# A fused attention and ternary-FFN layer: moving the weight-magnitude sums from the attention phase to ScalarE's queue in the projection phases, and reading the projection banks earlier

## The chip, the cores and the metric

The kernel runs as one program on all 8 cores of a Trainium2 chip. Each core works alone on its share of the tokens (1024 of 8192 query rows); the cores exchange nothing. The metric is the device time of the slowest core in microseconds (us).

## The reference, cut to what matters

`x` is 2 sequences of 4096 tokens with 2048 features, f32.

```python
xn = layernorm(x)
# attention, 16 heads of 128
q, k, v = xn @ Wq.T, xn @ Wk.T, xn @ Wv.T
q = layer_norm_per_head(q * gamma + beta) * 128**-0.5
k = layer_norm_per_head(k * gamma + beta)
attn = where(causal, (q @ k.T) ** 2, 0)
o = (attn @ v) / (attn.sum(-1) + EPS);  attn_out = o @ Wo.T
# FFN with ternary weights and int8-like activations
def bit_linear(x, w, g):
    xq = quantize(rms_norm(x, g))            # 127 / max|x| per row
    wq = clip(round(w / mean(|w|)), -1, 1) * mean(|w|)
    return xq @ wq.T
gate, up = split(bit_linear(xn, gate_w, 1));  h = silu(gate) * up
out = x + attn_out + bit_linear(h, down_w, 1)
```

The one scalar mean(|w|) of each FFN matrix must be known before its weights can be made ternary. That takes a pass over all of `gate_w` (23 M numbers) and `down_w` (11.5 M numbers): the kernel reads them in 264 chunks of 128 x 1024 f32 (512 KB each) and sums the absolute values of each chunk into a column of `wabs_g` or `wabs_d`. These chunks ("abs chunks" below) are what the change moves.

## The kernel before, in words

The program is written with raw engine queues. `V`, `SC` and `TE` (lines 159 to 168) append an instruction to VectorE (DVE), ScalarE (ACT) or TensorE (PE), and each engine runs its queue strictly in the order in which the Python code appended to it. Data passes by semaphores: `cV`, `cS` and `cT` count finished instructions of DVE, ACT and PE. So the order in the source is the schedule, by hand.

The phases, with a barrier between each:

- Phase 1 (32 tiles `t` of 128 tokens, the whole sequence). PE: 16 transposes of the normalised tile into `xnT` (`pe_transposes`, L339), the K projection (`proj_mm`, L364: 4 PSUM banks `kv_ps`, 16 matmuls of 128x512 each), 16 transposes of the K heads of the tile before (`head_transposes_store`, L416), and the V projection into the same four banks. K and V share the banks, so the V projection's first matmul waits until DVE has read bank 0 of K (L374, `kg <- kv_ps * gmb`), and the next K projection's banks are free when ACT has copied V out (L478).
- DVE and ACT in phase 1: `ln_tile` (L299 to L322) normalises tile t+1; `featuremap` (L374 to L400) reads the K banks, adds beta, makes squares on ACT (L380), the per-head statistics, a root on ACT (L393) and 16 scalings into `kfm`. The K heads' transposes are copied out alternately by ACT (L423) and DVE (L427) into two store buffers `ktb`, each of which must first have been stored to DRAM (`ksc`).
- `emit_abs(n)` (L264 to L285) takes the next n abs chunks: a DMA on POOL's queue into one of two buffers `wfp`, issued when that buffer's last reader has finished, and the sum, on ACT as an Abs with accumulation (L283, each followed by a read of the accumulator), or, with `dve=True`, on DVE as a reduction (L278). In phase 1 it is called twice a tile with 2 chunks: 4 a tile, 128 in all.
- Phase 2 (8 own tiles `s`): the same for Q with `wk_sb` reloaded with Wq, then an RMS norm and quantisation of the tile for the FFN (L544 to L568), stored through the same head transposes. `emit_abs` is called with 3, 3 and 2 chunks a tile: 64 in all.
- Phase 3: attention, for C = 0 (16 key blocks a head, all masked) and C = 1 (32 key blocks, the last 16 masked), over 16 heads. Per block: scores on PE (L642), the square on ACT (L653, or L664 unmasked), the mask on DVE (L655) if masked, and two matmuls (L670 for the output, L674 for the row sums). After each head ACT and DVE divide (L680, L683, L684), and then `emit_abs(3, dve=True)` stands on DVE's queue until the last 72 chunks are used: after the 16 heads of C = 0 and the first 8 of C = 1.
- Then Wo, gate and up with ternary weights, quantisation, and down. The change doesn't touch these.

Of the kernel before, what the change touches and what calls it, by code (L numbers as in the profile page):

```python
# [100 lines left out]
def build_nc():  # L101
# [57 lines left out]
    def V(fn, waits=(), drain=True):  # L159
        w = list(waits) + ([(cV, cV.n)] if drain else [])  # L160
        return b.op("vector", fn, waits=w, inc=cV)
# [5 lines left out]
    def TE(fn, waits=(), inc=True):  # L167
# [54 lines left out]
           for i in range(2)]  # L222
# [4 lines left out]
    wv_sb = es_wv.enter_context(nc.sbuf_tensor("wv_sb", [128, 16 * DM], BF16,  # L227
                                               side="right"))
# [35 lines left out]
    def emit_abs(n, dve=False):  # L264
        for _ in range(n):
            i = abs_i[0]
            if i >= len(abs_chunks):
                return
            abs_i[0] = i + 1
            src, which, col = abs_chunks[i]  # L270
            slot = i % 2
            en, val = abs_sc_ck[slot]
            b.dma("gpsimd", wfp[slot][:], src, s_abs[slot],
                  waits=[(CTR[en], val)])
            tgt = wabs_g if which == 0 else wabs_d
            if dve:
                abs_sc_ck[slot] = ("cV", V(
                    lambda e, sl=slot, t=tgt, cc=col: e.reduce_sum(  # L278
                        t[:, cc:cc + 1], wfp[sl][:], axis=AX.X,
                        apply_absolute_value=True), waits=[s_abs[slot]]))  # L280
            else:
                abs_sc_ck[slot] = ("cS", SC(
                    lambda e, sl=slot, t=tgt, cc=col: e.activation(  # L283
                        wabs_dump[:], wfp[sl][:], ACT.Abs,
                        accum_out=t[:, cc:cc + 1]), waits=[s_abs[slot]]))  # L285
# [83 lines left out]
            cks.append(cT.n)  # L369
        return cks  # L370

    def featuremap(dst_bf, q_scale, mm_cks, dst_waits):
        for j in range(4):
            v = V(lambda e, jj=j: e.tensor_tensor(  # L374
                kg[:, jj * 512:(jj + 1) * 512], kv_ps[jj][:],
                gmb[:, jj * 512:(jj + 1) * 512], ALU.mult),
                waits=[(cT, mm_cks[j]), (s_misc, ck_misc0)])
            st["kv_evac"][j] = ("cV", v)
        V(lambda e: e.tensor_add(kg[:], kg[:], btb[:]))  # L379
        sck = SC(lambda e: e.activation(kg2[:], kg[:], ACT.Square),  # L380
                 waits=[(cV, cV.n)])
        V(lambda e: e.reduce_sum(
            st1.ap().rearrange("p (h o) -> p h o", o=1),
            kg.ap().rearrange("p (h d) -> p h d", h=H), axis=AX.X))
        V(lambda e: e.reduce_sum(
            st2.ap().rearrange("p (h o) -> p h o", o=1),
            kg2.ap().rearrange("p (h d) -> p h d", h=H), axis=AX.X),
          waits=[(cS, sck)])
        V(lambda e: e.tensor_single_scalar(st1[:], st1[:], 1.0 / HD, ALU.mult))
        V(lambda e: e.tensor_single_scalar(st2[:], st2[:], 1.0 / HD, ALU.mult))  # L390
        V(lambda e: e.tensor_tensor(st3[:], st1[:], st1[:], ALU.mult))
        vck = V(lambda e: e.tensor_tensor(st2[:], st2[:], st3[:], ALU.subtract))
        sck = SC(lambda e: e.activation(st3[:], st2[:], ACT.Sqrt, bias=EPS),  # L393
                 waits=[(cV, vck)])
        V(lambda e: e.reciprocal(st3[:], st3[:]), waits=[(cS, sck)])
        if q_scale:
            V(lambda e: e.tensor_single_scalar(st3[:], st3[:], DSC, ALU.mult))
        last = 0
        for h in range(H):
            last = V(lambda e, hh=h, d=dst_bf: e.tensor_scalar(  # L400
                d[:, hh * 128:(hh + 1) * 128], kg[:, hh * 128:(hh + 1) * 128],
                st1[:, hh:hh + 1], st3[:, hh:hh + 1], ALU.subtract, ALU.mult),
                waits=(list(dst_waits) if h == 0 else ()), drain=(h == 0))
        return last
# [40 lines left out]
    kfm_ring = [kfm, kfm2]  # L445
# [4 lines left out]
    for t in range(NT):  # L450
        slot = t % 2
        if t + 1 < NT:
            nslot = (t + 1) % 2
            vf, sf = st["xf_free"][nslot]
            b.dma("sync", xf[nslot][:], xfull[(t + 1) * 128:(t + 2) * 128, :],
                  s_x[nslot], waits=[(cV, vf), (cS, sf)])
        pe_transposes(xnb[slot], [xnT[:, g * 512:(g + 1) * 512] for g in range(4)],
                      first_waits=[(cT, st["xnT_free"]), (cV, st["xn_ck"][t])])
        st["xnb_free"][slot] = [(cT, cT.n)]
        xnT_ready = [(cV, cV.n), (cS, cS.n)]  # L460
        kck = proj_mm(wk_sb, first_waits=[(s_w, ck_winit)] + xnT_ready)
        if pend1[0] is not None:
            pfm = pend1[0]
            head_transposes_store(kfm_ring[(t - 1) % 2], pfm,
                                  lambda h, tt=t - 1: ksc[h, :, tt, :])
            kfm_free2[(t - 1) % 2] = [(cT, cT.n)]
        emit_abs(2)
        if t + 1 < NT:
            st["xn_ck"][t + 1] = ln_tile(xf[(t + 1) % 2], want_f32=False,
                                         xslot=(t + 1) % 2)  # L470
        fm_ck = featuremap(kfm_ring[slot], q_scale=False, mm_cks=kck,
                           dst_waits=kfm_free2[slot])
        pend1[0] = fm_ck
        vck_banks = proj_mm(wv_sb, first_waits=[])
        st["xnT_free"] = vck_banks[-1]
        emit_abs(2)
        for j in range(4):
            v = SC(lambda e, jj=j, xs=slot: e.copy(  # L478
                xnb[xs][:, jj * 512:(jj + 1) * 512], kv_ps[jj][:]),
                   waits=[(cT, vck_banks[j])])  # L480
            st["kv_evac"][j] = ("cS", v)
        sck = cS.n
        for h in range(H):
            b.dma("sync", vsc[h, :, t, :], xnb[slot][:, h * 128:(h + 1) * 128],
                  s_kvw[slot], waits=([(cS, sck)] if h == 0 else []))
        st["xnb_free"][slot] = [(s_kvw[slot], s_kvw[slot].n)]
    head_transposes_store(kfm_ring[(NT - 1) % 2], pend1[0],
                          lambda h: ksc[h, :, NT - 1, :])
    kfm_free2[(NT - 1) % 2] = [(cT, cT.n)]
# [23 lines left out]
    for s in range(NOWN):  # L513
# [9 lines left out]
        xnT_ready = [(cV, cV.n), (cS, cS.n)]  # L523
        qck = proj_mm(wk_sb, first_waits=[(s_w, ck_wq)] + xnT_ready)
        st["xnT_free"] = qck[-1]
        emit_abs(3)
        if pend[0] is not None:
            pslot, pqb, pfm = pend[0]
# [8 lines left out]
        if s + 1 < NOWN:  # L537
            st["xn_ck"][s + 1] = ln_tile(xf[(s + 1) % 2], want_f32=True,
                                         xslot=(s + 1) % 2,
                                         xn_dst=xn_f[(s + 1) % 2])  # L540
        fm_ck = featuremap(kfm_ring[slot], q_scale=True, mm_cks=qck,
                           dst_waits=kfm_free2[slot])
        emit_abs(3)
        sck = SC(lambda e, xs=slot: e.activation(kg2[:], xn_f[xs][:],  # L544
# [23 lines left out]
        qb_ck = V(lambda e, xs=slot: e.tensor_copy(xnb[xs][:], xq8[:]),  # L568
                  waits=[(cT, xnT_tr_ck)])
        pend[0] = (slot, qb_ck, fm_ck)  # L570
        emit_abs(2)
    pslot, pqb, pfm = pend[0]
    head_transposes_store(kfm_ring[pslot], pfm,
                          lambda h: qsc[h, :, NOWN - 1, :])
# [43 lines left out]
    for C in range(2):  # L618
# [5 lines left out]
        for h in range(H):  # L624
# [62 lines left out]
                waits=[(cS, sck), (cT, zstop)])  # L687
            oz_free[h % 2] = vck
            rz_free = vck
            emit_abs(3, dve=True)  # L690

    assert abs_i[0] == len(abs_chunks), abs_i[0]

# [563 lines left out]
```

How the kernel before makes its waits and increments, by code:

```python
        def f(eng, wl=wl, fn=fn, ih=ih, inc_n=inc_n, drain=drain):  # L67
            for h, v in wl:
                if v > 0:
                    eng.wait_ge(h, v)
            if drain:
                eng.drain()
            ins = fn(eng)
            if ih is not None:
                ins.then_inc(ih, inc_n)
# [9 lines left out]
        def f(eng, wl=wl):  # L85
            for h, v in wl:
                if v > 0:
                    eng.wait_ge(h, v)
# [6 lines left out]
            def f(eng, h=bar.h, t=target):  # L95
                eng.sem_inc(h, 1)
                eng.wait_ge(h, t)
```

## Time and profile before

| what | value |
|---|---|
| median of the runs | 4940.29 us (4912.0 to 4968.58, 2 runs) |
| the profiled execution | 4851.61 us |
| its span (core 7, the slowest) | 4850.1 us |
| all cores' spans | 4817.5 to 4850.1 us |
| PE busy | 2984.8 us, 62% of the span |
| DVE busy | 1933.9 us, 40% |
| ACT busy | 1734.1 us, 36% |

The profile shows one execution on its slowest core. Busy shares are averages over phases with different limits, so the phases have to be read apart. In a line of the timeline the two first numbers are start and duration in us, then engine, line, operation and tiles, and in square brackets the idle time of that engine just before, with what ended it. PE matmuls are pipelined: 64 projection matmuls at TensorE's full clock take 13.97 us.

### The profile page before, as it was taken

To read this page: it belongs to the slowest core of one execution; us is meant where nothing else is said; L and a number is where in the kernel's file an instruction comes from. 1 tells how busy PE (TensorE), PEld (TensorE's weight loads), DVE (VectorE), ACT (ScalarE), POOL (GpSimd) and SP (SyncE) were. 2 spreads that over 40 slices of the span, in tenths; PEclk is the share of its full clock that TensorE was granted. 3 is DMA by queue.
4 is the path that set the end of the run, shared out by engine and by line. 5 is a ranking of instruction groups with operands and counts; after the bars stand their busy time and mean duration, and the time that the engine had idled before them with its cause. 6 is when DMAs were issued, how large, how long until landed. Compare 5 with 4: busy or idle time off the path is not lost.

```text
span 4850.1 us, 52075 instructions; the slowest of 8 cores (4817.5 to 4850.1 us)
## 1 busy us (share of the span) xinstructions
PE 2984.8 (62%) x13416; PEld 1244.3 (26%) x13416; DVE 1933.9 (40%) x3488; ACT 1734.1 (36%) x2541; POOL 241.1 (5%) x452
## 2 busy tenths in 40 slices
PE   0767676766767232332455567776899989313888
PEld 0333232333333111110111122222344434111333
DVE  0434444353443245443333233213366666332221
ACT  0322222232222123223333455552244444453551
POOL 1000000000000100000000000000000000000000
PEclk9988888888889665666778899998999999655999
DMA  9333333333333633223333323114477676445886
GB/s 173 84 94 88 92 92 83 94 89 96 88 87 84 146 89 98 76 85 107 93 92 95 112 96 117 56 56 131 141 233 235 230 229 201 145 148 170 285 283 188
DMA packets 312716, 628.19 MB, mean 130 GB/s; under 512 B 181872, under 2 KB 194160, under 8 KB 280432
## 3 DMA queue, kind: packets, MB, share of 16 engines
q0 software_dynamic: 64512, 310.41, 22.3%
q1 hardware_dynamic: 247920, 314.45, 21.0%
q8 instruction: 123, 2.02, 0.2%
q14 instruction: 161, 1.32, 0.1%
HBM read 573.34 MB, written 84.93 MB: 136 GB/s over the span
## 4 chain that ended last, share of the span: by engine, by line
PE 36%; DVE 19%; ACT 15%; DMA 13%; issue 10%; another core or an unknown queue 3%; SPq 3%; DVEq 1%; ACTq 1%; POOL 0%; POOLq 0%
PE kv_ps L364 19%; PE ops L670 4%; ACT s2t L653 3%; DMA xob<-xown 3%; DMA hgr<-hgscr 2%; SPq L80 2%; ACT sgn L758 2%; ACT sgn L761 2%; DVE s2t L655 2%; PE gps L909 2%; PE zps L674 2%; PE sps L642 2%; PE wops L830 2%; PE ups L921 2%
## 5 line engine op out<-in xcount | busy, mean ns | idle before, releaser
L364 PE MATMUL kv_ps<-wv_sb,xnT 128*128 128x512 bf16 x2048 | 516.3, 419 | 356.7 <-DVE kg L374 356.7
L364 PE MATMUL kv_ps<-wk_sb,xnT 128*128 128x512 bf16 x2560 | 579.4, 388 | 170.1 <-DMA wv_sb<-wvt 89.0
L670 PE MATMUL ops<-s2t,vsb 128*128 128x512 bf16 x768 | 304.5, 397 | 392.2 <-DVE s2t L655 342.6
L653 ACT ACTIVATE s2t<-sps 128x512 bf16<-128x512 f32 x512 | 305.8, 597 | 434.4 <-PE sps L642 422.7
L655 DVE TENSOR_TENSOR s2t<-s2t,msk_sb 128x512 bf16<-128x512 bf16 x512 | 217.4, 425 | 564.1 <-ACT s2t L653 559.8
L909 PE MATMUL gps<-terng,xqs 128*128 128x512 bf16 x1408 | 343.9, 401 | 74.3 <-DVE ternu L777 58.1
L364 PEld LDWEIGHTS kv_ps<-wv_sb,xnT 128*128 128x128 bf16 x2048 | 214.3, 106 | 648.5 <-issue 454.1
L364 PEld LDWEIGHTS kv_ps<-wk_sb,xnT 128*128 128x128 bf16 x2560 | 252.3, 100 | 485.2 <-issue 204.0
L427 DVE COPY sgn<-tp_ps 128x512 bf16<-128x512 bf16 x96 | 40.8, 424 | 842.3 <-PE tp_ps L416 592.1
L1134 PE MATMUL dps<-dtern,hqts 128*128 128x512 bf16 x1408 | 325.2, 394 | 65.7 <-DMA hqts<-hqtd 62.0
L642 PE MATMUL sps<-qsb,ksb 128*128 128x512 bf16 x768 | 304.6, 399 | 42.2 <-DMA qsb<-qsc 42.1
L423 ACT COPY sgn<-tp_ps 128x512 bf16<-128x512 bf16 x96 | 56.3, 586 | 761.8 <-PE tp_ps L416 573.1
L921 PE MATMUL ups<-ternu,xqs 128*128 128x512 bf16 x1408 | 318.3, 379 | 0.0
L674 PE MATMUL zps<-s2t,ones_bf 128*128 128x512 bf16 x768 | 306.2, 399 | 0.0
L283 ACT ACTIVATE sgn<-wfp 128x1024 bf16<-128x1024 f32 x192 | 203.0, 1057 | 215.7 <-DMA wfp<-gwt_r 184.9
L339 PE MATMUL tp_ps<-ident,xnb 128*128 128x128 bf16 x640 | 56.5, 236 | 362.1 <-ACT xnT L345 192.2
L670 PEld LDWEIGHTS ops<-s2t,vsb 128*128 128x128 bf16 x768 | 74.8, 97 | 667.2 <-issue 666.0
L909 PEld LDWEIGHTS gps<-terng,xqs 128*128 128x128 bf16 x1408 | 143.1, 102 | 262.5 <-issue 113.4
L1134 PEld LDWEIGHTS dps<-dtern,hqts 128*128 128x128 bf16 x1408 | 140.1, 101 | 250.6 <-issue 100.6
L1062 PE MATMUL tp<-ident,hgb 128*128 128x128 bf16 x352 | 51.3, 300 | 245.1 <-DVE hgb L1038 175.5
L80 POOL DMA_DIRECT2D wfp<-gwt_r x176 | 96.8, 553 | 1910.5 <-ACT sgn L283 1905.5
L380 ACT ACTIVATE kg<-kg 128x2048 f32<-128x2048 f32 x40 | 76.5, 1912 | 314.9 <-DVE kg L379 314.9
(139 smaller groups left out, 3597.3 us busy)
## 6 DMA issues: line engine op xcount, KB each, us to landing
wfp<-gwt_r POOLq DMA_DIRECT2D x176, 512.0 KB, 4.8
wfpt<-gwt_r POOLq DMA_DIRECT2D x88, 1024.0 KB, 6.1
wfp<-dwt_r POOLq DMA_DIRECT2D x88, 512.0 KB, 4.1
xqs<-xqsc SPq DMA_DIRECT2D x88, 512.0 KB, 4.3
wfpt<-dwt_r POOLq DMA_DIRECT2D x44, 1024.0 KB, 7.6
hqts<-hqtd SPq DMA_DIRECT2D x32, 1408.0 KB, 8.5
xf<-xfull SPq DMA_DIRECT2D x32, 1024.0 KB, 5.5
hgscr<-hgb SPq DMA_DIRECT2D x88, 256.0 KB, 2.4
```

What stands on the lines that cost most here:

```text
L80: return self.op(engine, lambda e, o=out, i=in_: e.dma_start(out=o, in_=i), waits=waits, inc=sem, inc_n=16)
L283: lambda e, sl=slot, t=tgt, cc=col: e.activation(wabs_dump[:], wfp[sl][:], ACT.Abs, accum_out=t[:, cc:cc + 1]), waits=[s_abs[slot]]))
L364: TE(lambda e, jj=j, f=fc, w=w_sb: e.matmul(kv_ps[jj][:], xnT[:, f * 128:(f + 1) * 128], w[:, f * DM + jj * 512: f * DM + (jj + 1) * 512], ...
L642: TE(lambda e, sl=slot, vv=v, bb=sb: e.matmul(sps[bb][:], ksb[sl][:, vv * 128:(vv + 1) * 128], qsb[sl][:], start=True, stop=True), waits=w ...
L653: sck = SC(lambda e, bb=sb: e.activation(s2t[bb][:], sps[bb][:], ACT.Square), waits=[(cT, mm_ck)])
L655: vck = V(lambda e, bb=sb, vv=v: e.tensor_tensor(s2t[bb][:], s2t[bb][:], msk_sb[:, (vv % 16) * 512:((vv % 16) + 1) * 512], ALU.mult), wait ...
L670: TE(lambda e, sl=slot, vv=v, bb=sb, hh=h, n=NC: e.matmul(ops_[hh % 2][:], vsb[sl][:, vv * 128:(vv + 1) * 128], s2t[bb][:], start=(vv == 0 ...
L674: TE(lambda e, vv=v, bb=sb, hh=h, n=NC: e.matmul(zps[hh % 2][:], ones_bf[:], s2t[bb][:], start=(vv == 0), stop=(vv == n - 1)), inc=(v == N ...
L758: SC(lambda e, w=wv: e.activation(sgn[0][:], w, ACT.Sign, bias=th_m[:, 0:1]), waits=[s_gw[slot], (cV, sgn_free[0])] + list(extra))
L909: TE(lambda e, f=fc, r=ring, bb=pb, xs=xslot: e.matmul(gps[bb][:], xqs[xs][:, f * 128:(f + 1) * 128], terng[r][:, f * 512:(f + 1) * 512], ...
L921: TE(lambda e, f=fc, r=ring, bb=pb, xs=xslot: e.matmul(ups[bb][:], xqs[xs][:, f * 128:(f + 1) * 128], ternu[r][:, f * 512:(f + 1) * 512], ...
L1134: TE(lambda e, f=fc, h_=hs, bb=pb, r=ring: e.matmul(dps[bb][:], hqts[h_][:, f * 128:(f + 1) * 128], dtern[r][:, f * 512:(f + 1) * 512], st ...
```

## The change

Three edits:

1. The reading of the four projection banks (L374) is split off from `featuremap` as `featuremap_evac`. In phase 1 it now stands on DVE's queue ahead of `ln_tile` of the next tile, in phase 2 directly behind the Q projection and ahead of the head transposes' copies.
2. The abs chunks of phase 1 become 6 a tile: the 2 ahead of `ln_tile` are gone, the 2 behind the V projection stay, and 4 are added at the end of the tile, behind the four V copies. In phase 2 they become 3, 3 and 3.
3. The 72 DVE sums in phase 3 are gone (32 x 6 + 8 x 9 = 264 is all of them).

```diff
-    def featuremap(dst_bf, q_scale, mm_cks, dst_waits):
+    def featuremap_evac(mm_cks):
         for j in range(4):
             v = V(lambda e, jj=j: e.tensor_tensor(
                 kg[:, jj * 512:(jj + 1) * 512], kv_ps[jj][:],
                 gmb[:, jj * 512:(jj + 1) * 512], ALU.mult),
                 waits=[(cT, mm_cks[j]), (s_misc, ck_misc0)])
             st["kv_evac"][j] = ("cV", v)
+
+    def featuremap(dst_bf, q_scale, dst_waits):
         V(lambda e: e.tensor_add(kg[:], kg[:], btb[:]))
...
# phase 1, tile t
-        emit_abs(2)
+        featuremap_evac(kck)
+        vck_banks = proj_mm(wv_sb, first_waits=[])
+        st["xnT_free"] = vck_banks[-1]
         if t + 1 < NT:
             st["xn_ck"][t + 1] = ln_tile(xf[(t + 1) % 2], want_f32=False,
                                          xslot=(t + 1) % 2)
-        fm_ck = featuremap(kfm_ring[slot], q_scale=False, mm_cks=kck,
+        fm_ck = featuremap(kfm_ring[slot], q_scale=False,
                            dst_waits=kfm_free2[slot])
         pend1[0] = fm_ck
-        vck_banks = proj_mm(wv_sb, first_waits=[])
-        st["xnT_free"] = vck_banks[-1]
         emit_abs(2)
...
         st["xnb_free"][slot] = [(s_kvw[slot], s_kvw[slot].n)]
+        emit_abs(2)
+        emit_abs(2)
# phase 2, tile s
         st["xnT_free"] = qck[-1]
+        featuremap_evac(qck)
         emit_abs(3)
...
         pend[0] = (slot, qb_ck, fm_ck)
-        emit_abs(2)
+        emit_abs(3)
# phase 3, end of a head
             rz_free = vck
-            emit_abs(3, dve=True)
```

PE's, SP's and POOL's queues hold the same instructions in the same order as before, but that POOL issues 192 of the abs loads ahead of the reload of `wk_sb`, not 128. Lines behind 374 are numbered 2 to 5 higher in the changed kernel.

ACT in phase 1, one tile from the root of `featuremap` (L393, then L395) to the root of the next tile's. L283 are the abs chunks, L478/L480 the V copies, L345 the copies of the transposed tile `xnT`, L423/L425 those of the K heads. Before:

```order
L393 ACTIVATE st<-st 128x16
L283 ACTIVATE sgn,wabs_g<-wfp 128x1024 x2
L478 CAST xnb<-kv_ps 128x512 x4
L345 COPY xnT<-tp_ps 128x512 x2
L423 COPY sgn<-tp_ps 128x512 x2
L283 ACTIVATE sgn,wabs_g<-wfp 128x1024 x2
L299 ACTIVATE xnb,lnst<-xf 128x2048
```

and in the changed kernel:

```order
L395 ACTIVATE st<-st 128x16
L283 ACTIVATE sgn,wabs_g<-wfp 128x1024 x2
L480 CAST xnb<-kv_ps 128x512 x4
L283 ACTIVATE sgn,wabs_g<-wfp 128x1024 x4
L345 COPY xnT<-tp_ps 128x512 x2
L425 COPY sgn<-tp_ps 128x512 x2
L299 ACTIVATE xnb,lnst<-xf 128x2048
```

Four chunks now stand between the V copies and the copies of `xnT`, on which the next K projection waits; none stands ahead of `ln_tile` (L299) any more.

DVE in phase 1, the same tile from the K heads' copies (L427, then L429) to the add of beta (L379, then L381). Before:

```order
L427 COPY sgn<-tp_ps 128x512 x2
L302 TENSOR_REDUCE lnst<-xf 128x1
...
L322 TENSOR_SCALAR xnb<-xf,lnst 128x2048
L374 TENSOR_TENSOR kg<-kv_ps,gmb 128x512 x4
L379 TENSOR_TENSOR kg<-kg,btb 128x2048
```

and in the changed kernel:

```order
L429 COPY sgn<-tp_ps 128x512 x2
L374 TENSOR_TENSOR kg<-kv_ps,gmb 128x512 x4
L302 TENSOR_REDUCE lnst<-xf 128x1
...
L322 TENSOR_SCALAR xnb<-xf,lnst 128x2048
L381 TENSOR_TENSOR kg<-kg,btb 128x2048
```

The four readings of the K banks have passed the seven instructions of `ln_tile`.

DVE in phase 3, C = 0, one head: L655 (then L660) are the 16 masks of a head, L684 (then L689) its division. Before:

```order
L655 TENSOR_TENSOR s2t<-s2t,msk_sb 128x512 x16
L684 TENSOR_TENSOR O_sb<-ops,sgn 128x512
L278 TENSOR_REDUCE wabs_d<-wfp 128x1 x3
```

and in the changed kernel:

```order
L660 TENSOR_TENSOR s2t<-s2t,msk_sb 128x512 x16
L689 TENSOR_TENSOR O_sb<-ops,sgn 128x512
```

The three sums between a head's division and the next head's first mask are gone.

## Rows read from the trace of the kernel before

**Rows 1.** Phases 1, 2, 3 (C = 0): busy PE, PEld, DVE, ACT, POOL, PEclk, DMA, GB/s.

```profile
117.00:1580.00 1463.00, 1021.11 (x5025) 466.19 (x5026) 646.01 (x1209) 424.76 (x655) 67.73 (x125) 0.87 0.33 89
...
1700.00:2200.00 500.00, 151.99 (x784) 73.56 (x784) 230.33 (x395) 138.78 (x218) 33.71 (x59) 0.62 0.30 87
2200.00:2716.00 516.00, 239.99 (x792) 65.47 (x792) 185.53 (x332) 178.63 (x298) 24.78 (x47) 0.78 0.31 93
```

**Rows 2.** The chain that ended last, four projections of 64 matmuls: start, duration.

```profile
151.39 13.97 PE kv_ps L364 x64
...
836.86 16.94 PE kv_ps L364 x64
...
1558.45 13.97 PE kv_ps L364 x64
...
1868.16 16.69 PE kv_ps L364 x64
```

**Rows 3.** Waits in phase 1: total us, times, longest us.

```profile
PE kv_ps L364 <- DVE kg L374: 356.7, 31, 13.2
```

**Rows 4.** The timeline of one tile of phase 1.

```profile
801.06 1.06 ACT L283 ACTIVATE sgn<-wfp 128x1024 bf16<-128x1024 f32 x1 [0.20 <-ACT st L393]
802.76 0.53 POOL L80 DMA_DIRECT2D wfp<-gwt_r  x1 [17.76 <-ACT sgn L283]
803.54 1.93 ACT L478 CAST xnb<-kv_ps 128x512 bf16<-128x512 f32 x3
806.60 0.59 ACT L478 CAST xnb<-kv_ps 128x512 bf16<-128x512 f32 x1 [1.12 <-PE kv_ps L364]
...
807.25 7.50 SPq L80 DMA_DIRECT2D vsc<-xnb  x16
807.38 0.59 ACT L345 COPY xnT<-tp_ps 128x512 bf16<-128x512 bf16 x1 [0.19 <-PE tp_ps L339]
...
809.67 13.97 PE L364 MATMUL kv_ps<-wk_sb,xnT 128*128 128x512 bf16 x64 [0.96 <-DVE xnT L349]
...
829.69 0.42 DVE L427 COPY sgn<-tp_ps 128x512 bf16<-128x512 bf16 x1 [4.93 <-DMA ksc<-sgn]
...
836.02 3.08 DVE L374 TENSOR_TENSOR kg<-kv_ps,gmb 128x512 f32<-128x512 f32 x4
...
836.86 13.47 PE L364 MATMUL kv_ps<-wv_sb,xnT 128*128 128x512 bf16 x48 [11.45 <-DVE kg L374]
...
847.55 0.22 ACT L393 ACTIVATE st<-st 128x16 f32<-128x16 f32 x1 [3.99 <-DVE st L392]
```

**Rows 5.** The timeline of tile 31, which has no `ln_tile` behind it.

```profile
1579.83 15.80 PE L364 MATMUL kv_ps<-wv_sb,xnT 128*128 128x512 bf16 x64 [5.63 <-DVE kg L374]
```

**Rows 6.** Abs loads, issue to landing: all of phase 1, then 829 to 833.

```profile
DMA to landing us min/median/max: 3.7/4.9/7.0
...
DMA to landing us min/median/max: 4.5/4.6/4.8
```

**Rows 7.** The timeline of one tile of phase 2.

```profile
1833.59 3.08 DVE L374 TENSOR_TENSOR kg<-kv_ps,gmb 128x512 f32<-128x512 f32 x4
...
1851.69 1.06 ACT L283 ACTIVATE sgn<-wfp 128x1024 bf16<-128x1024 f32 x1 [3.89 <-DMA wfp<-gwt_r]
...
1859.12 0.59 ACT L345 COPY xnT<-tp_ps 128x512 bf16<-128x512 bf16 x1
...
1861.36 1.06 ACT L283 ACTIVATE sgn<-wfp 128x1024 bf16<-128x1024 f32 x1 [0.20 <-DMA wfp<-gwt_r]
...
1866.05 0.42 DVE L349 COPY xnT<-tp_ps 128x512 bf16<-128x512 bf16 x1
```

**Rows 8.** The timeline at the end of a head of C = 0 in phase 3.

```profile
2357.66 2.54 DVE L278 TENSOR_REDUCE wabs_d<-wfp 128x1 f32<-128x1024 f32 x2
...
2364.78 0.95 DVE L655 TENSOR_TENSOR s2t<-s2t,msk_sb 128x512 bf16<-128x512 bf16 x2
...
2365.35 0.58 PE L670 MATMUL ops<-s2t,vsb 128*128 128x512 bf16 x1 [9.66 <-DVE s2t L655]
```

More of the change, by code:

```diff
@@ L540, in build_nc @@
                                          xn_dst=xn_f[(s + 1) % 2])
-        fm_ck = featuremap(kfm_ring[slot], q_scale=True, mm_cks=qck,
+        fm_ck = featuremap(kfm_ring[slot], q_scale=True,
                            dst_waits=kfm_free2[slot])
```

## The prediction

> **What bounds the kernel now.** I read the trace cut into phases first, then the waits of each phase, then the timeline of one tile or head of each. In the cut the reader should see that in none of the three phases that the change touches an engine is full: PE is busy for 1021 of 1463 us in phase 1, 152 of 500 in phase 2, 240 of 516 in the C = 0 part of phase 3, and the other engines are busy for less than half [rows 1]. These phases are bound by chains from engine to engine, so what matters is who stands in the chain of a tile, not how much work is moved.
>
> Phase 1: K projections start at 151.39 (tile 1) and 1558.45 (tile 31), 30 tiles apart [rows 2]: 1407.06 / 30 = 46.9 us a tile. PE's large wait is that of the V projection for the reading of the K banks, 356.7 us in 31 waits, 11.5 us each [rows 3]. The timeline of one tile [rows 4], counted from its K start at 809.67, shows the whole chain: K ends at 14.0; DVE's last copy of the K heads, held by the store of the buffer before, starts at 20.0; `ln_tile`; the bank readings at 26.35; V at 27.2; the root of `featuremap` at 37.9. The tile before shows what follows: two abs chunks (801.06), four V copies (from 803.54, the last held back to 806.60 by V's end), the first copy of `xnT` (807.38), and 2.29 us behind its start the next K. Today the root and the V end come almost together, and that is what the change upsets.
>
> **The change part by part, phase 1.**
>
> The early bank reading. Behind the same late head copy (20.0, ends at 20.44) L374 now comes at once, and V starts at about 21.4. Tile 31 has no `ln_tile` and shows this: V at 1579.83, 21.38 after its K, with 5.63 us of idle PE instead of 11.45 [rows 5, 4]. V starts 5.8 us earlier.
>
> Does that end the tile earlier? Only if V's end is what is waited for. DVE still has the same work from the head copy to the root (`ln_tile`, four readings, the add, two reductions, the small ones); only the order differs. So the root stays at 847.55 - 809.67 = 37.9; that ACT does `ln_tile`'s square sooner, with no chunks ahead of it, gives at most a few tenths, and I take 0.25. V meanwhile ends at 21.4 + 16.9 = 38.3 at the latest (16.94 us for a V behind a long idle time [rows 2]). The V copies stand on ACT's queue behind the root and two chunks. The chain now runs over DVE and ACT alone, and the 5.8 us are slack for PE. I value the early reading at 0.25 us a tile.
>
> The chunks behind the V copies. Call the start of the first chunk behind the root 0. Two chunks take 2.48 (801.06 to 803.54), four V copies 1.93 + 0.65 = 2.6, so they end at 5.05. Four more chunks follow, from two buffers. A buffer's next load is issued 1.70 behind the start of its chunk (801.06 to 802.76), and lands about 4.5 later (4.5 to 4.8 for the pair issued amid the K stores, 3.7 to 7.0 over phase 1 [rows 6]). So each chunk can start 6.2 behind the last one of its buffer: the third at 6.2, the fourth at 7.45, the fifth at 12.4, the sixth at 13.65. The sixth ends, its accumulator read, at 14.9. Only then comes the first copy of `xnT`, at 15.0, and the next K at 17.3. What is queued behind on ACT are the copies of `xnT`, for which PE's transposes wait, and behind these K. The chunks that left the place ahead of `ln_tile` give nothing back: ACT idled there.
>
> The clock. PE now idles from V's end to the next K but for a few transposes, about 17 us. The granted clock shows in the durations: after 0.96 us of idleness 64 matmuls took 13.97 us; after long waits 16.94 (V here) and 16.69 (Q in phase 2, with transposes just ahead of it, as K will have) [rows 2, 4]. TensorE's two levels are 1.2 and 2.4 GHz, and the long waits put the first matmuls on the lower. So K takes 16.7 instead of 13.97: +2.7 a tile, and this is on the path. V's slow start goes from the path.
>
> A tile is then 16.7 (K) + (37.9 - 14.0 - 0.25 = 23.65, K's end to the root) + 0.3 (root to first chunk) + 17.3 = 57.95; I say 57.9, against 47.3 for this tile (809.67 to V at 836.86, which repeats with the next K 20.1 behind it). Difference 10.6. 31 intervals from K to K: 31 x 10.6 = 329. Behind tile 31 the head stores queue behind the V stores anyhow (7.50 us of issuing on SP [rows 4]); with the slower K I put 5 there. Phase 1: **+334 us**.
>
> **A load time that only a page has.** The pair of loads in the rows took 4.5 to 4.8 us. The Trainium skill, in "DMA: Bandwidth & Descriptors", section "Anatomy of one DMA — SWDGE (gpsimd) path", gives a fit of about 2.0 us plus the bytes over 436 GB/s; for 512 KB that is an estimate of 3.2 us, and the two loads in the chain would make the tile 2.6 us shorter and phase 1 81 us less slow. The trace disagrees with it by over a microsecond, and no load here landed before 3.7, so the sum keeps 4.5.
>
> **Phase 2.** Here DVE's chain sets the tile: its last instructions for the quantisation end just before it copies `xnT` (1866.05), while ACT had its first copy of `xnT` ready at 1859.12 [rows 7]. Moving L374's four readings (3.08 us) under the Q projection takes 3.1 us off that chain, with the waits for the third chunk (3.89 us) kept, since these run from ACT's own times. Seven tiles (the first one's readings are early already): -22. One chunk more stands ahead of ACT's copy of `xnT`. Its data would land where the first chunk of the next set now starts, 1861.36, minus the 3.1: it ends at 1859.5, the copy starts at 1859.6, and DVE's own copy would come at 1862.95. It is covered by 3 us; without that cover it would cost up to 1.25 + 3.9 a tile, 8 x 5.15 = 41. Phase 2: **-22 us**, between -22 and +19.
>
> **Phase 3.** At the end of a head of C = 0 DVE takes three sums, the third after a wait for its load, and the next head's first mask comes at 2364.78 where it could come at 2357.66: 7.1 us, and PE waits 9.66 [rows 8]. That happens behind 15 heads; behind the 16th the new mask is being loaded, and in C = 1 the first 16 blocks of a head need no mask. 15 x 7.1 = 107. PE would idle for some 2.5 us there instead of 9.66, so part of the slow start may go too; its bounds are 0 and the 2.97 us that it costs a projection (16.94 - 13.97). The block there is a loop over ACT and DVE with PE only partly in it, so I stand near the lower end: 0.5 a head, 8. Phase 3: **-115 us**, between -107 and -152.
>
> **The sum.** +334 - 22 - 115 = +197. Against the profiled execution: 4851.6 + 197 = 5048.6 us, 4.1% slower. That execution is 88.7 us below the median of the two runs shown (4940.29); on that median the same difference gives 5137, and the range has to hold this.
>
> **Rivals.**
>
> Loads too early to be waited for (no measurable change). If the loads were in the buffers when the four chunks come, these would cost 5.0 us of ACT, not 9.9: a tile is 10.6 - 4.9 = 5.7 longer, 31 x 5.7 = 177, net 177 + 5 - 22 - 115 = +45: 4897. For it: POOL is idle and loads at once when a buffer is free. Against it: with two buffers a load cannot be issued before its predecessor is summed, and in phase 2 the third chunk of a set waits 3.89 us [rows 7]. A faster landing alone (3.7) gives 1.6 less a tile, net +147.
>
> Slower still: the four loads now fly while SP issues the 16 V stores (7.50 us of issuing [rows 4]). The page "DMA: Bandwidth & Descriptors" of the Trainium skill says in "Issuing engines are not separate DMA queues" that DMAs of all issuing engines share the same 16 and interleave. The trace has loads of up to 7.0 [rows 6]. If that were usual, two loads in a chain give 2 x 2.5 = 5 a tile, +155: 5204. Against: the pair issued amid the K stores landed in 4.5 and 4.8.
>
> The other side: V's end leads (faster). If DVE and ACT had room, so that root, V copies and chunks all fit ahead of V's end, the tile would shrink by V's 5.8 us: 31 x 5.8 = 180, net -180 - 22 - 115 = -317: 4535. It decides at the last V copy: the change is faster if the sixth chunk ends before V does. For it: the 11.5 us wait is PE's largest. Against it: that needs the root 15 us ahead of V's end, and it stands at 37.6 against 38.3.
>
> **How the numbers follow.** Forecast +197 with chance 0.80: its own range goes from a tile of +9.0 with phase 3 at its best (279 + 5 - 22 - 152 = +110, 4962) to +13 with phases 2 and 3 at their worst (403 + 5 + 19 - 107 = +320, 5172). No change 0.08; much slower 0.08; faster 0.04. A change below about 2% (97 us) can't be told from none by a measurement of this kernel. The likeliest case reaches just above that line, so slower gets 0.87, within 2% 0.09, faster 0.04. Range 4955 to 5170, which also takes in the median's offset.
>
> **What would show it.** Right: K starts some 57 to 58 us apart in phase 1; ACT's fifth chunk of a tile waiting 4 to 5 us for its load; PE's transposes waiting on ACT's copy of `xnT`; V starting 21 to 24 us behind K with a wait of about 6 us; K taking over 16 us; C = 0 heads about 22 us apart instead of 30. Wrong: K starts under 50 us apart, or ACT's V copies waiting for PE, which would mean that V's end leads.

## The result, and the profile after

The changed kernel takes 5136.93 us (median of 11 runs, 5114.16 to 5184.15), the kernel before 4903.9 us (median of 10). The ratio is 1.0525, 95% interval 1.0476 to 1.0575: slower, as forecast, and by more than the forecast's 4.1%. In the profiled executions the median span of the eight cores went from 4834.4 to 5098.8 us, +264. In some executions of any kernel the four cores of a die run together at a lower granted clock and take some per cent longer; the two medians include such runs, the ratios and the comparisons below leave them, or those cores, out.

The waits in phase 1 of the changed kernel (columns: total us, times, longest), which answer to [rows 3]:

```profile
PE tp_ps L339 <- ACT xnT L345: 521.8, 30, 20.7
...
ACT sgn L283 <- DMA wfp<-gwt_r: 219.4, 114, 4.5
PE kv_ps L364 <- DVE kg L374: 169.9, 30, 6.2
```

The wait for the bank reading has halved (356.7 to 169.9 us), as the change set out to do. A wait nearly three times the saving of 187 us has come up: the transposes wait 17.4 us a tile for ACT's copies of `xnT`. ACT itself waits 219 us for the loads of abs chunks, of which nothing showed before. The timeline of one tile, which answers to [rows 4]:

```profile
1139.24 16.66 PE L364 MATMUL kv_ps<-wk_sb,xnT 128*128 128x512 bf16 x64 [0.96 <-DVE xnT L349]
...
1161.94 0.43 DVE L429 COPY sgn<-tp_ps 128x512 bf16<-128x512 bf16 x1 [4.92 <-DMA ksc<-sgn]
...
1163.38 16.54 PE L364 MATMUL kv_ps<-wv_sb,xnT 128*128 128x512 bf16 x64 [5.70 <-DVE kg L374]
...
1179.64 0.21 ACT L395 ACTIVATE st<-st 128x16 f32<-128x16 f32 x1 [3.99 <-DVE st L394]
1179.95 1.06 ACT L283 ACTIVATE sgn<-wfp 128x1024 bf16<-128x1024 f32 x1
...
1182.42 2.60 ACT L480 CAST xnb<-kv_ps 128x512 bf16<-128x512 f32 x4
...
1186.99 1.06 ACT L283 ACTIVATE sgn<-wfp 128x1024 bf16<-128x1024 f32 x1 [1.96 <-DMA wfp<-gwt_r]
...
1188.47 1.06 ACT L283 ACTIVATE sgn<-wfp 128x1024 bf16<-128x1024 f32 x1 [0.33 <-DMA wfp<-gwt_r]
...
1193.22 1.06 ACT L283 ACTIVATE sgn<-wfp 128x1024 bf16<-128x1024 f32 x1 [3.61 <-DMA wfp<-gwt_r]
...
1195.54 1.06 ACT L283 ACTIVATE sgn<-wfp 128x1024 bf16<-128x1024 f32 x1 [1.17 <-DMA wfp<-gwt_r]
...
1196.77 0.59 ACT L345 COPY xnT<-tp_ps 128x512 bf16<-128x512 bf16 x1
1197.50 1.01 PE L339 MATMUL tp_ps<-ident,xnb 128*128 128x128 bf16 x8 [16.61 <-ACT xnT L345]
```

Read it downward from the root at 1179.64: two chunks, the four V copies, then four chunks each behind a wait for its load, and only then the copy of `xnT` for which PE has waited since V ended, but for eight transposes. "K to K", the distance from the start of one K projection to that of the next, is 60.2 us here (the next K starts at 1199.47).

The stages of the changed kernel, answering to [rows 1] (us, then PE, PEld, DVE, ACT and POOL busy, PE clock, DMA share, GB/s):

```profile
117.00:1980.00 1863.00, 1092.55 (x4964) 487.48 (x4963) 647.08 (x1207) 490.27 (x771) 100.61 (x186) 0.78 0.31 87
2100.00:2610.00 510.00, 167.42 (x851) 80.21 (x849) 249.74 (x417) 155.72 (x244) 41.82 (x69) 0.63 0.33 97
2640.00:2980.00 340.00, 215.83 (x733) 59.00 (x732) 114.09 (x259) 165.23 (x275) 0.00 (x0) 0.91 0.15 49
```

Phase 1's granted clock (in parts of full speed) went from 0.87 to 0.78, that of the C = 0 attention from 0.78 to 0.91. POOL issues nothing in the attention any more.

From the starts of matmuls and divisions on all eight cores (medians over the cores, us):

| stretch | before | after | difference | forecast |
|---|---|---|---|---|
| K of tile 0 to K of tile 1 | 33.4 | 51.6 | +18.2 | +10.6 |
| K of tile 1 to K of tile 31 | 1405.3 | 1787.9 | +382.6 | +318 |
| K of tile 31 to first Q | 119.5 | 120.9 | +1.4 | +5 |
| Q of tile 0 to Q of tile 1 | 48.5 | 54.3 | +5.8 | 0 |
| Q of tile 1 to Q of tile 7, to the first division | 422.9 + 117 | 404.5 + 107 | -28 | -22 |
| attention, C = 0 | 448 | 334 | -114 | -115 |
| attention, C = 1, and all behind | 2124 | 2119 | -5 | 0 |
| sum | | | +261 | +197 |

### The profile page after: what moved, and what is told of

Its sections match the earlier page's. It is cut to its first block, busy times and chain, and to the rows that moved or that the text cites. A ratio compares the mean times of both kernels' runs of the same rounds, so it can differ in the third digit from the quotient of the medians.

```text
span 5136.3 us, 52147 instructions; the slowest of 8 cores (5079.6 to 5136.3 us)
## 1 busy us (share of the span) xinstructions
PE 3067.2 (60%) x13416; PEld 1272.4 (25%) x13416; DVE 1847.3 (36%) x3416; ACT 1815.6 (35%) x2685; POOL 245.2 (5%) x452
## 4 chain that ended last, share of the span: by engine, by line
PE 28%; DVE 22%; DMA 18%; ACT 14%; issue 11%; SPq 3%; another core or an unknown queue 2%; DVEq 1%; ACTq 1%; POOLq 0%; POOL 0%
PE kv_ps L364 13%; DMA wfp<-gwt_r 6%; PE ops L675 3%; SPq L80 3%; DMA xob<-xown 3%; ACT s2t L658 3%; DVE s2t L660 2%; ACT sgn L762 2%; ACT sgn L765 2%; PE dps L1138 2%; PE zps L679 2%; PE sps L647 2%; DMA hgr<-hgscr 2%; DVE kg L381 2%
## 5 line engine op out<-in xcount | busy, mean ns | idle before, releaser
L364 PE MATMUL kv_ps<-wk_sb,xnT 128*128 128x512 bf16 x2560 | 647.8, 420 | 165.0 <-DMA wv_sb<-wvt 88.1
L339 PE MATMUL tp_ps<-ident,xnb 128*128 128x128 bf16 x640 | 69.5, 271 | 857.2 <-ACT xnT L345 716.0
L660 DVE TENSOR_TENSOR s2t<-s2t,msk_sb 128x512 bf16<-128x512 bf16 x512 | 217.7, 425 | 628.7 <-ACT s2t L658 623.9
L283 ACT ACTIVATE sgn<-wfp 128x1024 bf16<-128x1024 f32 x264 | 278.9, 1056 | 374.6 <-DMA wfp<-gwt_r 219.4
L364 PEld LDWEIGHTS kv_ps<-wk_sb,xnT 128*128 128x128 bf16 x2560 | 268.9, 106 | 534.9 <-issue 293.3
L1138 PE MATMUL dps<-dtern,hqts 128*128 128x512 bf16 x1408 | 332.8, 400 | 66.6 <-DMA hqts<-hqtd 57.9
L425 ACT COPY sgn<-tp_ps 128x512 bf16<-128x512 bf16 x96 | 56.3, 586 | 795.0 <-PE tp_ps L418 622.0
L429 DVE COPY sgn<-tp_ps 128x512 bf16<-128x512 bf16 x96 | 40.8, 425 | 786.6 <-PE tp_ps L418 535.4
L339 PEld LDWEIGHTS tp_ps<-ident,xnb 128*128 128x128 bf16 x640 | 51.7, 121 | 881.9 <-issue 881.9
L374 DVE TENSOR_TENSOR kg<-kv_ps,gmb 128x512 f32<-128x512 f32 x160 | 110.7, 692 | 272.8 <-PE kv_ps L364 240.5
```

The source lines that it names most:

```text
L283: lambda e, sl=slot, t=tgt, cc=col: e.activation(wabs_dump[:], wfp[sl][:], ACT.Abs, accum_out=t[:, cc:cc + 1]), waits=[s_abs[slot]]))
L339: TE(lambda e, bb=bank, f=fc, jj=j, s=src_bf: e.transpose(bb[:, jj * 128:(jj + 1) * 128], s[:, f * 128:(f + 1) * 128], ident[:]), waits=wl ...
L364: TE(lambda e, jj=j, f=fc, w=w_sb: e.matmul(kv_ps[jj][:], xnT[:, f * 128:(f + 1) * 128], w[:, f * DM + jj * 512: f * DM + (jj + 1) * 512], ...
L660: vck = V(lambda e, bb=sb, vv=v: e.tensor_tensor(s2t[bb][:], s2t[bb][:], msk_sb[:, (vv % 16) * 512:((vv % 16) + 1) * 512], ALU.mult), wait ...
L1138: TE(lambda e, f=fc, h_=hs, bb=pb, r=ring: e.matmul(dps[bb][:], hqts[h_][:, f * 128:(f + 1) * 128], dtern[r][:, f * 512:(f + 1) * 512], st ...
```

## The experiments

Each of these is the changed kernel or the kernel before with one thing different. K to K is given as the mean from tile 1 to tile 31 and over the cores: 46.8 before, 59.6 in the changed kernel. The root is the ACT instruction L393 (L395) of `featuremap`, with which ACT's part of a tile's chain begins. The tail is the four chunks at the end of a tile.

**The early reading alone.** Sums as in the kernel before.

```diff
# against the changed kernel
+        emit_abs(2)
         featuremap_evac(kck)
...
-        emit_abs(2)
-        emit_abs(2)
```

> The kernel before with the early bank reading alone (phases 1 and 2); all sums where they were. Theory A (a tile of phase 1 is set by the chain over DVE and ACT, root, two chunks, V copies, xnT copies, so the early V is slack): V starts about 21.4 us behind K instead of 27.2, but K to K stays 46 to 47 us; phase 2 gives about 20 us; whole kernel 20 to 35 us faster, ratio 0.993 to 0.996. Theory B (V's end leads, PE's largest wait is worth its length): K to K 41 us, 180 us faster in phase 1, ratio about 0.96.

Ratio to before 1.003, interval 1.000 to 1.006; K to K 47.9. Theory B is out: V starts 23.3 us behind K instead of 27.4, and the tile is no shorter. But theory A's small gain failed too: the tile got 1.1 us longer, and the kernel was not the 20 to 35 us faster that were expected. The timeline of one tile:

```profile
1017.40 15.80 PE L364 MATMUL kv_ps<-wk_sb,xnT 128*128 128x512 bf16 x64 [0.96 <-DVE xnT L349]
...
1041.63 15.64 PE L364 MATMUL kv_ps<-wv_sb,xnT 128*128 128x512 bf16 x64 [6.66 <-DVE kg L374]
...
1057.89 0.22 ACT L395 ACTIVATE st<-st 128x16 f32<-128x16 f32 x1 [3.99 <-DVE st L394]
```

K takes 15.80 us where it took 13.97 [rows 2]. V now ends while DVE and ACT are still busy, so PE is idle ahead of K (8.5 us on the mean from V's end to K's start, transposes included, against 3.3), and K begins at the lower clock. The granted clock over K and over its first 5.6 us (the number ahead of the last two):

```profile
1017.40:1033.20 15.80, 15.80 (x67) 6.79 (x68) 0.00 (x0) 0.00 (x0) 0.00 (x0) 0.88 0.33 93
1017.40:1023.00 5.60, 5.60 (x18) 2.16 (x19) 0.00 (x0) 0.00 (x0) 0.00 (x0) 0.67 0.29 63
```

and over the K of [rows 4], in the kernel before:

```profile
809.67:823.64 13.97, 13.97 (x67) 6.42 (x68) 0.00 (x0) 0.00 (x0) 0.00 (x0) 1.00 0.35 106
```

K's mean length over the tiles is 15.8 us against 14.0 (here and below on the cores whose traces hold all 64 matmuls of K). K is on the path, V is not: the idle time was moved from where it was free to where it costs. The rest of the way adds up: from the root to the first copy of `xnT` it is 0.9 us less (5.5 against 6.4), since the V copies no longer wait for V's end, and from there to K 0.4 more.

**The moved sums alone.** The bank reading late, as before.

```diff
-        featuremap_evac(kck)
-        vck_banks = proj_mm(wv_sb, first_waits=[])
...
+        featuremap_evac(kck)
         fm_ck = featuremap(kfm_ring[slot], q_scale=False,
                            dst_waits=kfm_free2[slot])
+        vck_banks = proj_mm(wv_sb, first_waits=[])
```

> The changed kernel with the bank reading late, as before; the sums where the change puts them. Theory A: K to K within 1.5 us of the changed kernel's 60.2, since V's end, 47 us behind K, comes only just behind the root and its two chunks; with phase 2's 20 us given back the ratio to before is 1.055 to 1.065. Theory B (the early reading hides part of the tail and without it the tile is 5.8 us longer): K to K 66, ratio about 1.09.

Ratio 1.0591, interval 1.0491 to 1.0691; K to K 59.6, the same as in the changed kernel. V starts 29.1 us behind K instead of 23.4 and it makes no difference: theory A. (The difference to 1.0525 is within the intervals; phase 2's gain is gone too, Q of tile 0 to tile 7 in 469 us against 459.)

**The tail left out.** The changed kernel without the four chunks at the end of a tile of phase 1.

```diff
         st["xnb_free"][slot] = [(s_kvw[slot], s_kvw[slot].n)]
-        emit_abs(2)
-        emit_abs(2)
```

> The changed kernel without the four tail chunks of each tile of phase 1; 128 of the 264 chunks are left out of the sums. Theory A: K to K is 45.3 us if K keeps the high clock behind the shorter wait, 48 if not; the tail's whole price is then 12 to 15 us a tile, and the ratio to before 0.96 to 0.985. Theory E (the tail is not what lengthened the tile): K to K stays above 55.

K to K 47.9, the same as with the early reading alone: the tail's whole price is 11.7 us a tile. The best run took 4753.94 us against 4853.35 of the kernel before on the same chip, 0.980. Of the two values expected, 48 for a slow K came true (K takes 15.9 us here); the price was expected at 12 to 15.

**Half of the tail unloaded.**

```diff
+        emit_abs(2)
+        emit_abs(2, load=False)   # sums the buffers as they are
```

> The changed kernel, but the last two of a tile's four tail chunks are summed from what is in the buffers, with no load of their own; their weights are left out of the sum. Theory A (each tail chunk costs its sum and the wait for its load): the fifth chunk starts right behind the fourth, which takes 4 to 4.5 us off a tile, K to K 56, ratio to before about 1.023. Theory E (loads are not waited for, the clock or PE sets the tile): K to K stays 60.

K to K 54.8, 4.8 us under the changed kernel's, where 4 to 4.5 were expected; the best run took 4972.96 us against 4853.35, 1.025. The sixth chunk starts 11.3 us behind the root instead of 15.8. The tail in this run (core 1; lines are one higher here):

```profile
1036.76 1.06 ACT L284 ACTIVATE sgn<-wfp 128x1024 bf16<-128x1024 f32 x1 [0.52 <-DMA wfp<-gwt_r]
...
1039.46 1.06 ACT L284 ACTIVATE sgn<-wfp 128x1024 bf16<-128x1024 f32 x1 [1.56 <-DMA wfp<-gwt_r]
...
1040.70 1.06 ACT L284 ACTIVATE sgn<-wfp 128x1024 bf16<-128x1024 f32 x1
...
1041.94 1.06 ACT L284 ACTIVATE sgn<-wfp 128x1024 bf16<-128x1024 f32 x1
```

The last two follow at once, 1.24 us apart, where with loads they waited. So of the tail's 11.7 us a tile, 4 x 1.24 = 5.0 are the sums and the rest, 6.7, are waits for loads, 4.8 of them for the second pair. (The changed kernel's list of waits above has 219.4 us in 30 tiles, 7.3 a tile.)

**Attention without the sums.** The kernel before, its 72 sums on DVE left out.

```diff
-            emit_abs(3, dve=True)
```

> The kernel before without the 72 sums on DVE in phase 3, which are left out. Theory A: the heads of C = 0 come 22.2 us apart instead of 29.9, those of C = 1 as before; 115 us less, ratio to before 0.976. Rival (the sums hide beside the attention's own loop and the changed kernel's shorter phase 3 has another cause): heads 28 us apart or more, ratio above 0.99.

Heads of C = 0 come 22.3 us apart instead of 29.8; the attention's C = 0 part takes 335 us against 448, and the 16 heads of C = 1 take 580 against 581. Best run 4720.41 against 4853.35, 0.973. The rival is out, and this accounts for 113 of the changed kernel's -114. Two divisions of this run:

```profile
2306.45 0.69 DVE L684 TENSOR_TENSOR O_sb<-ops,sgn 128x512 bf16<-128x512 f32 x1 [2.50 <-ACT sgn L683]
2328.85 0.69 DVE L684 TENSOR_TENSOR O_sb<-ops,sgn 128x512 bf16<-128x512 f32 x1 [2.50 <-ACT sgn L683]
```

**What makes the loads late.** The mean starts of a tile's six chunks behind the root are 0.3, 1.6, 6.2, 8.7, 12.5 and 15.8 us; the forecast had 0.3, 1.6, 6.5, 7.8, 12.7 and 14.0. So it is the second load of each pair that is late. Three runs looked for what holds it back.

First, V stored in one DMA of 4 KB rows instead of 16 DMAs of 256-byte rows; the layout differs, so phase 3 reads other numbers of V:

```diff
-        for h in range(H):
-            b.dma("sync", vsc[h, :, t, :], xnb[slot][:, h * 128:(h + 1) * 128],
-                  s_kvw[slot], waits=([(cS, sck)] if h == 0 else []))
+        b.dma("sync", vsc_w[t], xnb[slot][:], s_kvw[slot], waits=[(cS, sck)])
```

> The changed kernel with V stored by one DMA a tile in rows of 4 KB instead of 16 DMAs in rows of 256 bytes; same bytes, but in another layout, so phase 3 reads other numbers of V. Theory C (the tail's loads land late because they share the DMA engines with the V stores' small rows): median landing in phase 1 falls from 5.2 to about 4.5 us, and with two landings in a chain K to K falls from 60.2 to 58.5 or 59, 40 to 55 us in all, ratio to before about 1.043. Theory D (they land late because all cores now load in bursts, or because loads follow one another closely): landing stays 5.2, K to K stays at 60, ratio 1.052.

Slower, not faster: ratio 1.0641 (1.0563 to 1.0719), K to K 60.9. The gain of theory C did not come, and D did not foresee a loss. The timeline (core 4) shows what moved:

```profile
1005.31 0.32 SPq L80 DMA_DIRECT2D vsc<-xnb  x1
1005.79 0.33 SPq L80 DMA_DIRECT2D xf<-xfull  x1
1008.14 1.06 ACT L283 ACTIVATE sgn<-wfp 128x1024 bf16<-128x1024 f32 x1 [2.90 <-DMA wfp<-gwt_r]
```

The 16 V stores keep SP busy for 8 us, and with one store the 1 MB load of the next tile is issued 0.5 us behind it, into the tail. That gave a new theory, tried by holding the tile load back:

```diff
             b.dma("sync", xf[nslot][:], xfull[(t + 1) * 128:(t + 2) * 128, :],
-                  s_x[nslot], waits=[(cV, vf), (cS, sf)])
+                  s_x[nslot], waits=[(cV, vf), (cS, sf)] + xnT_ready)
```

> The changed kernel, but the 1 MB load of the next tile waits for the copies of xnT, so that it flies while K runs (as it did before the change, when SP came to it some 5 us behind K's start) and not beside the tail's last two loads. Theory F (the tail's loads are late because this load falls among them): the sixth chunk starts 14.3 us behind the root instead of 15.8, K to K falls from 59.5 to about 58, 40 us in all. Theory G (two loads in flight at a time slow each other, whoever else loads): no change beyond 0.3 us a tile.

> The changed kernel with both: V stored by one DMA a tile in rows of 4 KB (another layout, so phase 3 reads other numbers of V), and the 1 MB tile load late. Against the run with the late load alone this prices the V stores' small rows by themselves. Theory C (small rows hold the loads back): K to K 1 to 1.5 us under that run. Theory G: the same as that run; the wide store's own slower tile, 60.9, came from the tile load that followed it at once.

With the tile load late: ratio 1.0546 (1.0473 to 1.062), K to K 59.2, sixth chunk at 15.5 us: 0.4 us a tile, where theory F wanted 1.5; single cores of one execution lie up to 1.2 us apart, so that 0.4 is hardly clear of nothing. With both: K to K 58.9, against 59.2 on the same cores with the late load alone. So the tile load hurts when it falls among the tail's loads (the wide store's 60.9 became 58.9 by delaying it), but in the changed kernel it hardly does.

The 0.3 us of the last step is what is left of two larger effects. The times from issue to landing show them; means over tiles and cores, and in brackets how far behind the load ahead of it a load was issued:

| run | first | second | third | fourth |
|---|---|---|---|---|
| kernel before (two loads behind the root) | 4.0 | 5.3 (1.4) | | |
| changed kernel | 4.1 | 5.1 (1.3) | 4.5 (4.5) | 5.2 (2.6) |
| tile load late | 3.9 | 5.1 (1.3) | 4.5 (4.5) | 4.9 (2.7) |
| wide V store, tile load late | 4.0 | 5.6 (1.3) | 4.3 (4.6) | 4.2 (3.1) |

The wide store made the second load 0.5 slower and the fourth 0.7 faster. Of the fourth load's 5.2 us in the changed kernel, 0.3 are the tile load's. In the last run neither this nor a V store is in flight beside it, and there it lands in 4.2; but it is also issued 3.1 us behind the third and not 2.7, and these runs don't part the two. So theory C holds at most for the fourth load.

The second load is late by the first. No run had one load in flight at a time, but the kernel before has such loads. Take all its abs loads, on all cores and behind the first 150 us, and keep those beside which no DMA of their core but abs loads was in flight. With no earlier load in flight the median landing is 3.9 us (353 loads). Issued less than 2 us behind one that is still in flight, it is 4.9 (139 loads). Issued 3 us or more behind it, it is 3.9 again (307). With V stores in flight the first two values are 4.0 and 5.2. One such pair of phase 2, issued at 1847.12 and 1848.36, and what the core's queues carried from 1846 to 1854:

```profile
DMA to landing us min/median/max: 4.4/4.4/4.4
DMA to landing us min/median/max: 5.1/5.1/5.1
q0 software_dynamic: 288, 1.05, 42.0%
```

The 288 packets with 1.05 MB are the pair's, and no other queue shows. So a load close behind another takes about 1 us longer. This is a comparison of loads within one execution and not an experiment, and what the other cores loaded meanwhile is not held fixed.

**The sums elsewhere.** Four chunks behind the copies of `xnT`, while K runs, and two ahead of `ln_tile`.

```diff
         kck = proj_mm(wk_sb, first_waits=[(s_w, ck_winit)] + xnT_ready)
+        emit_abs(4)
...
+        emit_abs(2)
         featuremap_evac(kck)
...
         pend1[0] = fm_ck
-        emit_abs(2)
...
-        emit_abs(2)
-        emit_abs(2)
```

> The changed kernel with phase 1's six chunks elsewhere on ACT's queue: four behind the copies of xnT, where ACT idles while K runs, two ahead of ln_tile, none between the root and the next K. Theory A: nothing of the sums is in the chain of a tile; K to K is about 43 us if K runs at the high clock and 45.7 if at the low one, against 46.9 before; with phase 3's 115 us and phase 2's 20 the ratio to before is 0.945 to 0.965. Rival: the sums' loads now fly amid the K head stores and hold the head copies back; K to K 47 or more, ratio 0.97 to 0.975.

Ratio 0.9758 (0.9654 to 0.9861): faster than both kernels, though against the kernel before the interval reaches into gains below 2%. The same 264 sums by the same engine now hide. K to K is 47.3, not the 43 to 45.7 expected, and the ratio missed 0.965 too: the first copy of `xnT` comes at 43.2 us, as it should, but K another 4.1 behind it. DVE's copies of `xnT` stand behind the 16 scalings of `featuremap` (4.19 us) and had been hidden by the chunks and V's end. The rival had named just these numbers, 47 and 0.97 to 0.975, but its mechanism is not there: the head copies are not held back, for from K's end to the root it is 23.8 us here and 23.8 in the changed kernel. K itself takes 16.4 us.

> The sums under K and ahead of ln_tile as in the run before, but phase 1's bank reading back behind ln_tile as in the kernel before. Theory A with the clock (the early V only leaves PE idle ahead of K, whose matmuls then start at the lower clock): K runs in 13.8 us, K to K 46.5 to 47.0, tile 0 takes 33 to 34 us again, and the ratio to before is 0.970 to 0.975, no slower than with the early reading (0.976). Rival (early reading helps once the chunks are out of the way): K to K 48 or more, ratio 0.985.

This run puts the bank reading back behind `ln_tile` (the diff of the second experiment on top of the one above). Ratio 0.971 (0.9632 to 0.9789), K to K 46.9, and K takes 13.97 us again:

```profile
1000.07 13.97 PE L364 MATMUL kv_ps<-wk_sb,xnT 128*128 128x512 bf16 x64 [0.96 <-DVE xnT L349]
...
1005.79 1.06 ACT L283 ACTIVATE sgn<-wfp 128x1024 bf16<-128x1024 f32 x1 [3.68 <-DMA wfp<-gwt_r]
...
1027.82 16.09 PE L364 MATMUL kv_ps<-wv_sb,xnT 128*128 128x512 bf16 x64 [12.00 <-DVE kg L374]
...
1044.27 0.61 PE L339 MATMUL tp_ps<-ident,xnb 128*128 128x128 bf16 x8 [0.37 <-PE kv_ps L364]
```

PE's 12 us wait ahead of V is back, a chunk waits 3.68 us for its load, and neither costs anything: the transposes follow V by 0.37 us. The early reading of phase 1 is worth nothing here. Neither is a tile of phase 1 any shorter than the kernel before's 46.8: what this kernel gains, it gains in phases 2 and 3. One part missed: tile 0 takes 42 us and not 33 to 34, since all six chunks of tile 0 stand ahead of the square of `ln_tile` on ACT, each pair waiting for its loads, and V waits with `ln_tile` for them (V at 138.58, 23.2 us behind K's start, where it followed K at once before).

The last run keeps the early reading and moves DVE's two copies of `xnT` to ACT:

```diff
-            if g % 2 == 0:
+            if True:
                 v = SC(lambda e, bb=bank, d=dsts[g]: e.copy(d, bb[:, 0:512]),
```

> The sums under K with the early reading, and all four copies of xnT on ACT instead of two on DVE, where they stand behind the 16 scalings of featuremap (phase 1) or the whole quantisation (phase 2). Theory H (with the tail gone DVE's copy of xnT is the last wait ahead of K): K to K falls from 47.3 to 45.5 or 46.3, a tile of phase 2 by about 4 us, ratio to before 0.955 to 0.965. Rival (ACT's copies, one behind the other, take as long): K to K 47, ratio 0.975.

Ratio 0.9663 (0.9587 to 0.9739), the lowest of all, though just above the 0.955 to 0.965 expected, and its interval overlaps those of the two runs before it: K to K 46.0, and a tile of phase 2 1.6 us shorter than in the two runs before it. Theory H holds in phase 1. In phase 2 4 us were expected: Q still waits for the counter of DVE's last instruction, the quantisation's cast, whoever copies `xnT`:

```profile
1837.97 1.23 DVE L572 CAST xnb<-xq 128x2048 bf16<-128x2048 int8 x1
1839.55 15.63 PE L364 MATMUL kv_ps<-wk_sb,xnT 128*128 128x512 bf16 x64 [1.72 <-DVE xnb L572]
```

## Why the prediction was right, and where it was off

The direction, the mechanism and the chain were right. +197 us (4.1%) was forecast and 5.25% measured, inside the range. The +264 of the spans lie inside the sum's own range, +110 to +320, too, so the room left for the median's offset was not needed.

- **"I value the early reading at 0.25 us a tile."** Right that it is slack, shown by the first two experiments; K's end to the root fell from 24.2 to 23.8 us. But it isn't a gain by itself: with the sums where they were it costs 1.1 us a tile, by the clock. The forecast had that price (K at 16.7, +2.7), but laid it at the door of the tail alone. K's mean is 16.0 against 14.0 in the changed kernel, so the term was +2.0.
- **The chunks behind the V copies: the term that was mis-sized.** The step that failed is "lands about 4.5 later", taken for both loads of a pair. It rested on one pair in a tile that was looked at closely, while the same group of rows had a median of 4.9 over phase 1 [rows 6]. The two tail loads that decide, the second of each pair, took 5.1 and 5.2 us. For the second this isn't the change's doing: behind the root of the kernel before, the two loads of a tile already took 4.0 and 5.3 (means over tiles and cores). One such pair there, issued at 849.6 and 850.8:

```profile
DMA to landing us min/median/max: 4.1/4.1/4.1
DMA to landing us min/median/max: 4.7/4.7/4.7
```

  From the second chunk's sum to the fourth's, and from the fourth's to the sixth's, it was therefore 7.1 us and not 6.2: 0.6 to 0.7 of the longer landing, and 0.2 from the landing to the start of the sum, which the forecast left out. Twice in a chain, this makes the way from the root to the first copy of `xnT` 17.0 us on the mean, forecast as 15.3. With 0.5 more from that copy to K and 0.6 less from K to the root (K took 16.0, not 16.7), a tile is 59.6 and not 57.9. And the difference counts against a mean of 46.8 before, not against the 47.3 of the tile that was read. 12.75 in place of 10.6, 64 us over 30 tiles, is the largest part of the gap between +197 and +264.
- **The first tiles: a term that was missing.** Tile 0 lost 18.2 us, 7.6 more than forecast, and the first tile of phase 2 lost 5.8. In the kernel before, DVE did the reduction of tile 1's `ln_tile` at 29 us while PE waited for weights, and the rest, down to L322, while PE still ran K of tile 0; now all of it stands behind the last of the bank readings, which need the projection to be done. On DVE in the changed kernel:

```profile
122.51 0.69 DVE L374 TENSOR_TENSOR kg<-kv_ps,gmb 128x512 f32<-128x512 f32 x1 [93.33 <-PE kv_ps L364]
...
133.68 2.29 DVE L302 TENSOR_REDUCE lnst<-xf 128x1 f32<-128x2048 f32 x1
...
139.26 2.29 DVE L381 TENSOR_TENSOR kg<-kg,btb 128x2048 f32<-128x2048 f32 x1
```

  and in the kernel before:

```profile
29.13 2.29 DVE L302 TENSOR_REDUCE lnst<-xf 128x1 f32<-128x2048 f32 x1
...
124.89 1.35 DVE L322 TENSOR_SCALAR xnb<-xf,lnst 128x2048 bf16<-128x2048 f32 x1
...
134.98 2.29 DVE L379 TENSOR_TENSOR kg<-kg,btb 128x2048 f32<-128x2048 f32 x1
```

  In the run with the early reading alone tile 0 takes 39.8 us against 33.4, so 6.4 of the 18.2 come from it. With the moved sums alone, whose reading is late, the first Q spacing is 49 us, as before (48.5); in all runs with the early reading in phase 2 it is 52 to 56.
- **Phase 2, -22.** The other tiles gave 3.1 us each as worked out (422.9 to 404.5 over six tiles), and the extra chunk is covered. That the total is -22 as well is partly luck: the first tile lost 5.8, and the stretch from the last Q to the first division became 9 us shorter, of which the forecast explains 3. Where the other 6 come from was not looked into.
- **Phase 3, -115.** Measured -114, and the spacing of heads fell from 29.84 to 22.27: 7.6 a head, where 7.1 and 0.5 for the clock were forecast. The run without the sums gives the same.
- **Rivals.** Loads in time was out (114 waits for loads in phase 1). Loads stretched by the V stores was the right kind of error, late loads, but at most half of the cause: the fourth load took 5.2 us beside V's stores and the tile load and 4.2 without them, while the second is late by the first and took 0.5 more with wide rows. All told wide rows shortened the tile by 0.3 us at most. V's end leading was out. It also could not have come out as it was priced: the four tail chunks stand on ACT behind the last V copy, and that waits for V's end, so the sixth chunk cannot end before V does.
- **The chances.** "The likeliest case reaches just above that line" misreads the sum: +197 us is twice the 97 us of the line.

## What to carry to other kernels

Work that hides somewhere is not free wherever its engine has idle time: look up which instruction comes next on that queue and who waits for it. The same four sums a tile cost 11.7 us at the end of the tile and nothing that shows where ACT idles under a projection. A large wait in the list is worth what comes off the last chain, here nothing; removing it can move PE's idle time in front of a matmul group that is on the path, where the lower clock then costs. And a load's time taken from one pair was too short here: take the mean over the stage, and the second of two loads in flight apart from the first.

## What the runs showed of the hardware that was not expected

Two loads of 512 KB issued 1.3 and 2.6 us apart landed, in the changed kernel, 4.1 and 4.5 us (the first of each pair) and 5.1 and 5.2 us (the second) behind their issue, and storing V in wider rows made the second load slower by 0.5 us and the fourth faster by 0.7. In the kernel before, where no other DMA of the core was in flight, a load less than 2 us behind another took 4.9 us against 3.9.

The 64 matmuls of K took 14.0 us where V had ended 3.2 us before K began (transposes of `xnT` included; kernel before). They took 16.2 us behind 5.9 us (the last run), 16.4 behind 7.0, 15.8 behind 8.4 (the early reading alone), 16.1 behind 14.4 (the moved sums alone) and 16.0 behind 19.8 (the changed kernel). Among these, a longer wait did not make K longer.
